# Weighted sums of a key chunk issued in two pieces of 224 queries

## The chip, the cores and the metric

The kernel runs on one core of one Trainium2 chip. The metric is device time of one whole launch in microseconds. Three runs of the kernel before gave 10486.84, 10486.08 and 10497.13 us; the median is 10486.84 us. A chip profile of one execution comes with it.

## The reference, cut to what matters

Eight images of 128 channels and 56 x 56 pixels go through three blocks, each added to its input:

- group norm, a 7 x 7 neighbourhood attention with 16 heads, and a projection;
- layer norm over channels, a full attention over all 3136 pixels with 8 heads of 16, and a projection;
- layer norm, and two small matrices (one dequantized from 4-bit codes).

The change touches only the second:

```
scores  = einsum('bhqd,bhkd->bhqk', q, k) * scale
weights = softmax(scores)
attn    = einsum('bhqk,bhkd->bhqd', weights, v)      # the "weighted sums"
```

For each image, head and query there are 3136 keys.

## The kernel before, in words

Everything is written for one core with an explicit instruction stream for each engine, ordered by semaphores. The body of the image loop is unrolled but for the strips of the neighbourhood attention.

**Units and chunks.** The full attention of an image is cut into 14 units: 2 groups of 4 heads, times 7 blocks of 448 queries. In a unit, the keys go by in 25 chunks (0 to 24) of 128 keys, the last of 64. TensorE does three kinds of work in a chunk, each with four column tiles of 32 that run side by side:

- A *score group* (`scores_turned`, L747), one for each of the 4 heads: keys on the partitions, 448 queries as columns, bf16 operands with 99 rows. It goes to one of 3 PSUM banks (6 in the last unit). Below, scores 0 to 3 are those of heads 0 to 3.
- A *maximum tile* (`max_tile`, L684), for the unit after: 448 columns, bf16, 96 rows. VectorE reduces it over the keys (`take_max`, L1112). There are 98 for a unit, so 4 in most chunks and 3 in chunks 8 and 20. Units before the last but one have them in all chunks, the last but one up to chunk 20, the last has none.
- The *weighted sum* (`weigh`, L725) of the chunk before: fp32, 128 keys as rows, 32 value columns, 448 queries as columns, one matmul for each head, each in its own column tile. A matmul in fp32 leaves two records in the trace, here called its first and its second pass. All four accumulate in PSUM bank 6 over the 25 chunks.

ScalarE takes the exponential of every score group (L937, one instruction for each head and chunk) into a buffer that the weighted sum reads. `exp_done` counts these. A score group waits until the exponential three groups earlier is done, since it takes that one's bank (L743); the first of a unit waits for every exponential of the unit before. The weighted sum waits for all four exponentials of its chunk (L721).

**Order on TensorE in a chunk of four maximum tiles** (L766 to L777): maximum 0, scores 0, maximum 1, scores 1, maximum 2, scores 2, weighted sum of the chunk before, maximum 3, scores 3. The place of the weighted sum is `weigh_at = 2` (L735), and 3 in the last unit.

**Work between chunks.** After chunk 1 TensorE spreads the sums of the unit before (`spread`, L711), after chunk 3 it projects that unit (`project`, L715), both fp32 and 448 columns; in chunk 0 ScalarE reads the finished sums (`read_sums`, L911) once `pv_done` says so, between the exponentials of heads 1 and 2. At chunk 21 VectorE finishes the maxima of the next unit (L1117) and TensorE turns them (`turn_maxima`, L705).

Of the kernel before, what the change touches and what calls it, by code (L numbers as in the profile page):

```python
# [18 lines left out]
BLK = 448  # L19
# [18 lines left out]
PRIMED = 8  # L38
# [5 lines left out]
GH = 4  # L44
GROUPS = AHEADS // GH
CHUNKS = -(-TOK // P)
# [19 lines left out]
def max_steps(c):  # L66

    at = (c - MAX_CHUNKS) % CHUNKS
    return range(-(-MAXES * at // CHUNKS), -(-MAXES * (at + 1) // CHUNKS))
# [60 lines left out]
def hybrid_block(nc, images, x, consts, qkv_wT, rpb, proj_wT, proj_b, Wq, bq, Wk, bk, Wv, bv, Wo, bo,  # L130
# [3 lines left out]
    with ExitStack() as ctx:  # L134
# [3 lines left out]
        def sem(name):  # L138
            return ctx.enter_context(nc.semaphore(name))
# [30 lines left out]
        def part(at, n, dt=F32):  # L170
            v = arena[:, at:at + n]
            return v if dt == F32 else v.bitcast(dt)
# [4 lines left out]
        VA = part(22208, 6400).rearrange("p (c h e) -> p c h e", c=CHUNKS, h=AHEADS)  # L177
# [25 lines left out]
        PS = ctx.enter_context(nc.psum_tensor("PS", [P, 8, 512], F32))  # L203
# [35 lines left out]
        st_ready, exp_done, pv_done = sem("st_ready"), sem("exp_done"), sem("pv_done")  # L239
        attn_read, sums_spread, attn_normed, attn_proj, x_updated = (  # L240
            sem("attn_read"), sem("sums_spread"), sem("attn_normed"), sem("attn_proj"),
            sem("x_updated"))
# [13 lines left out]
        def wait_parts(eng, b, g):  # L256

            eng.wait_ge(high_parts_in[g], (b + 1) * (16 * GH * len(HIGH_ROWS)))
            apart(eng)
            eng.wait_ge(parts_in[g], (b + 1) * (16 * GH * (2 * len(Q_PARTS) - len(HIGH_ROWS))))  # L260
# [9 lines left out]
        def apart(eng):  # L270


            eng.sem_inc(paced, 1)
# [5 lines left out]
        def unit_index(b, unit):  # L279
            g, i = unit  # L280
            return b * AUNITS + (g * NBLK + i)
# [4 lines left out]
        def unit_queries(unit, h, at=0, n=BLK):  # L286

            start = (unit[1] * GH + h) * BLK + at
            return slice(start, start + n)

        def attention_units(body):

            def unit_at(k):
                return (k // NBLK, k % NBLK) if 0 <= k < AUNITS else None

            for k in range(AUNITS):
                body({d: unit_at(k + d) for d in (-1, 0, 1, 2)})

        def exp_buffer(c):
            return PB[2 if c == CHUNKS - 1 else c % 2]  # L300

        LAST_UNIT = (GROUPS - 1, NBLK - 1)
# [253 lines left out]
        def _(pe):  # L556
            mm = nc.tensor.matmul
# [7 lines left out]
            with pe.Fori(0, images) as b:  # L565

                for n in range(2):
                    pe.wait_ge(gn_cols, b * 3 + (n + 1))
                    mm(PS[:, 7, n:n + 1], group_w, gn[:, 3 * n:3 * n + 1], start=True,
                       stop=True).then_inc(block_ready, 1)  # L570
# [7 lines left out]
                for j in range(NBLK):  # L578
                    wait_freed(pe, b, NK, j)
                    for c in range(4):  # L580
                        t0 = (4 * j + c) * VROW
                        m = mm(PS[0:VROW, j, c * P:(c + 1) * P], XN[:, t0:t0 + VROW], W_qkv[:, 2 * P:3 * P],
                               start=True, stop=True)
# [84 lines left out]
                for j in range(NBLK):  # L668
                    wait_freed(pe, b, AK, j)
                    for c in range(4 * j, min(4 * j + 4, CHUNKS)):  # L670
                        n = LAST if c == CHUNKS - 1 else P
                        m = mm(PS[0:n, j, (c % 4) * P:(c % 4 + 1) * P], XN[:, c * P:c * P + n], W_v[:, :],
                               start=True, stop=True)
# [15 lines left out]
                def score_for_max(unit, m):  # L689

                    u = unit_index(b, unit)
                    bank, read = max_banks()[0][m]
                    if read is not None:
                        pe.wait_ge(max_read, u * MAXES + (read + 1))
                    elif bank != 7:

                        second = unit == (0, 1)
                        last = MAXES - 1 if second else max_banks()[1][bank]
                        pe.wait_ge(max_read, u * MAXES + (last + 1 - MAXES))
                    max_tile(unit, m, bank)  # L700

                def turn_maxima(unit):
                    pe.wait_ge(row_max_in, unit_index(b, unit) + 1)
                    apart(pe)
                    nc.tensor.transpose(PS[0:QTILES, 7, 0:P], row_max[:, :], ident).then_inc(max_turned, 1)  # L705

                def spread(unit):

                    pe.wait_ge(attn_read, unit_index(b, unit) + (1 + PRIMED))
                    pe.wait_ge(x_updated, unit_index(b, unit) + PRIMED)  # L710
                    mm(PS[:, 7, 0:BLK], pick_sum, tail[:, 0, :], start=True, stop=True).then_inc(sums_spread, 1)  # L711

                def project(unit):
                    pe.wait_ge(attn_normed, unit_index(b, unit) + 1)
                    mm(PS[:, 7, 0:BLK], W_o[:, unit[0], :], normed[:, :], start=True,  # L715
                       stop=True).then_inc(attn_proj, 1)

                def weigh(unit, c):

                    e = unit_index(b, unit)  # L720
                    pe.wait_ge(exp_done, e * (GH * CHUNKS) + (GH * c + GH + PRIMED))  # L721
                    if c == 0:
                        pe.wait_ge(attn_read, e + PRIMED)
                    for h in range(GH):
                        m = mm(PS[32 * h:32 * h + 32, 6, 0:BLK], VA[:, c, unit[0] * GH + h, :],  # L725
                               exp_buffer(c)[:, h, :], start=(c == 0), stop=(c == CHUNKS - 1),
                               tile_position=(0, 32 * h))
                    m.then_inc(pv_done, 1)

                def attention_unit(units):  # L730
                    unit, after, before = units[0], units[1], units[-1]
                    e = unit_index(b, unit)
                    g = unit[0]

                    weigh_at = 2 if after is not None else GH - 1  # L735

                    def scores_turned(c, h):

                        n = LAST if c == CHUNKS - 1 else P
                        at = c * GH + h  # L740
                        banks = ST_BANKS if after is not None else ALL_ST_BANKS

                        pe.wait_ge(exp_done, e * (GH * CHUNKS) + ((at + 1 - banks if at else 0) + PRIMED))  # L743
                        if n < P:
                            apart(pe)
                        for k0 in range(0, n, 32):
                            ins = mm(PS[k0:k0 + 32, at % banks, 0:BLK], KP[0:ROWSM, g, h, c * P + k0:c * P + k0 + 32],  # L747
                                     QP[0:ROWSM, g, unit_queries(unit, h)], start=True, stop=True,
                                     tile_position=(0, k0))
                        ins.then_inc(st_ready, 1)  # L750

                    for c in range(CHUNKS):
                        later = units[1 if c < MAX_CHUNKS else 2]
                        steps = list(max_steps(c)) if later is not None else []
                        if c == MAX_CHUNKS and later is not None and later[0] != g:
                            wait_parts(pe, b, later[0])
                        if c == TAIL_DONE and before is not None and after is not None:
                            pe.wait_ge(x_updated, e + PRIMED)
                            apart(pe)

                        def maxima(n):
                            for m in steps[:n]:
                                score_for_max(later, m)
                            del steps[:n]

                        maxima(1)  # L766
                        if c == 0:

                            pe.wait_ge(shift_in, (e + 1) * (16 * 3) + 16 * PRIMED)
                        for h in range(GH):  # L770
                            scores_turned(c, h)
                            if h == weigh_at and c > 0:
                                weigh(unit, c - 1)
                            if h == weigh_at and c == 0 and before is not None:
                                weigh(before, CHUNKS - 1)
                            maxima(1)
                        maxima(len(steps))  # L777
                        if c == SPREAD_AT and before is not None:
                            spread(before)
                        if c == PROJECT_AT and before is not None:  # L780
                            project(before)
                        if c == MAX_CHUNKS and after is not None:
                            turn_maxima(after)
# [11 lines left out]
                turn_maxima((0, 0))  # L795
                pe.wait_ge(v_ones, b * 3 + 3)
                attention_units(attention_unit)
                weigh(LAST_UNIT, CHUNKS - 1)
                spread(LAST_UNIT)
                project(LAST_UNIT)  # L800

# [381 lines left out]
```

## Time and profile before

| | |
|---|---|
| median of three runs | 10486.84 us |
| profiled execution, its own time | 10482.69 us |
| its span, first to last instruction | 10480.6 us |
| TensorE matmul busy | 8999.7 us (86%) |
| VectorE busy | 8033.9 us (77%) |
| ScalarE busy | 6604.5 us (63%) |
| mean granted TensorE clock | 0.916 |

Times are microseconds from the start of the span. Busy time of TensorE counts a matmul until its modelled end, so that neighbours overlap in the records; the distance between starts tells how fast the engine goes. The queries also give "PEld", the weight loads, which overlap the matmuls. Attention units fill about 830 us of the roughly 1303 us of an image.

### The profile page before, as it was taken

Reading aid. Unit: us, or ns where it says so; the run is one execution under the profiler, and the core shown is the slowest. Engines: PE = TensorE matmul, PEld = TensorE weight load, DVE = VectorE, ACT = ScalarE, POOL = GpSimd, SP = SyncE. Lnnn points to the kernel's source line nnn. Section 1 sums busy time; section 2 is a strip of 40 time slices with the busy share of each in tenths; the row PEclk is TensorE's granted clock in tenths of the full one; section 3 lists DMA queues with packets and bytes.
Section 4 is the critical chain, followed back from the end, with each engine's and each line's share of the span. In section 5 each row is a group of like instructions: output and inputs, shape, how many; then the busy total and the mean of one; then the engine's idle time right before and its main releaser. Section 6 shows DMA issues by size and latency. Waiting matters only on the chain.

```text
span 10480.6 us, 426471 instructions
## 1 busy us (share of the span) xinstructions
PE 8999.7 (86%) x166082; PEld 4883.0 (47%) x166082; DVE 8033.9 (77%) x13861; ACT 6604.5 (63%) x13585; POOL 1650.4 (16%) x1701
## 2 busy tenths in 40 slices
PE   5699967999679996799967999679996799967999
PEld 4344453444544545444453444534445344453444
DVE  5699757997579975799757996579965799657996
ACT  3388833888338883388833888338883388734887
POOL 5200042000410004100041000410004100051000
PEclk8799987999879998799987999879998799987999
DMA  3400034000330003300033000430004300033000
GB/s 62 63 3 3 3 57 62 3 3 3 59 60 3 3 3 60 59 3 3 3 61 58 3 3 3 62 57 3 3 3 63 56 3 3 6 60 55 3 3 9
DMA packets 386155, 269.61 MB, mean 26 GB/s; under 512 B 49836, under 2 KB 377244, under 8 KB 383516
## 3 DMA queue, kind: packets, MB, share of 16 engines
q1 hardware_dynamic: 378524, 229.58, 14.0%
q0 software_dynamic: 6144, 19.28, 1.2%
q8 instruction: 1046, 17.14, 0.7%
q14 instruction: 441, 3.61, 0.1%
HBM read 144.03 MB, written 25.86 MB: 16 GB/s over the span
## 4 chain that ended last, share of the span: by engine, by line
PE 65%; issue 20%; POOL 5%; DVE 3%; SPq 3%; ACT 2%; POOLq 1%; DMA 1%; ACTq 0%; DVEq 0%
PE PS L684 21%; PE PS L747 19%; PE PS L725 19%; POOL arena L477 2%; POOL arena L467 2%; SPq L408 2%; DVE block_max L1144 2%; ACT arena L937 1%; PE PS L653 1%; PE PS L715 1%; PE PS L711 1%; PE PS L657 1%; PE PS L574 1%; PE PS L648 1%; SPq L416 0%
## 5 line engine op out<-in xcount | busy, mean ns | idle before, releaser
L1112 DVE TENSOR_REDUCE block_max<-PS 128x1 f32<-128x448 f32 x10192 | 5687.8, 617 | 494.2 <-PE PS L684 361.4
L937 ACT ACTIVATE arena<-PS 128x448 f32<-128x448 f32 (+1 forms) x11200 | 5262.6, 560 | 1161.2 <-PE PS L747 1134.2
L684 PE MATMUL PS<-KP,arena 96*32 96x448 bf16 x43904 | 4142.4, 373 | 354.5 <-DMA KP<-arena 281.0
L747 PE MATMUL PS<-arena,KP 99*32 99x448 bf16 x43904 | 4033.8, 354 | 108.3 <-ACT arena L937 73.6
L725 PE MATMUL PS<-arena 128*32 128x448 f32 x22400 | 2648.9, 540 | 19.3 <-ACT arena L937 14.8
L684 PEld LDWEIGHTS PS<-KP,arena 96*32 96x32 bf16 x43904 | 1294.7, 98 | 2024.4 <-issue 531.7
L747 PEld LDWEIGHTS PS<-arena,KP 99*32 99x32 bf16 x43904 | 1275.9, 96 | 1632.1 <-ACT arena L937 884.1
L853 ACT ACTIVATE arena<-PS 80x512 f32<-80x512 f32 (+1 forms) x896 | 442.9, 537 | 1315.1 <-PE PS L613 1312.1
L613 PE MATMUL PS<-C,arena 128*80 128x128 f32 x3136 | 582.4, 361 | 675.1 <-POOL arena L477 675.1
L526 POOL CAST shift_parts<-shift 14x128 bf16<-14x128 f32 x112 | 31.3, 279 | 5427.7 <-ACT shift L903 5427.7
L725 PEld LDWEIGHTS PS<-arena 128*32 128x32 f32 x22400 | 714.0, 110 | 360.4 <-ACT arena L937 90.6
L613 PEld LDWEIGHTS PS<-C,arena 128*80 128x80 f32 x3136 | 456.9, 155 | 751.8 <-issue 716.6
L1040 DVE TENSOR_TENSOR arena<-PS,C 128x448 f32<-128x448 f32 x224 | 139.6, 623 | 705.9 <-PE PS L623 705.8
L602 PE MATMUL PS<-arena 32*32 32x80 f32 x25088 | 528.7, 235 | 109.3 <-issue 47.9
L477 POOL TENSOR_TENSOR arena<-arena 128x1120 f32<-128x1120 f32 x224 | 461.7, 2061 | 757.3 <-DVE arena L1035 757.3
L602 PEld LDWEIGHTS PS<-arena 32*32 32x32 f32 x25088 | 484.8, 108 | 138.9 <-issue 133.2
L1144 DVE TENSOR_REDUCE block_max<-PS 128x2 f32<-128x896 f32 x336 | 388.3, 1234 | 170.4 <-PE PS L684 170.4
L472 POOL TENSOR_TENSOR arena<-arena 128x1120 f32<-128x1120 f32 x224 | 461.3, 2060 | 355.8 <-DVE arena L1029 355.8
L903 ACT ACTIVATE shift<-PS 14x128 f32<-14x128 f32 x112 | 28.0, 250 | 686.3 <-PE PS L705 686.3
L1024 DVE TENSOR_TENSOR arena<-PS,nat_bias 128x80 f32<-128x80 f32 (+3 forms) x1120 | 353.9, 382 | 119.9 <-PE PS L602 88.5
L1127 DVE TENSOR_TENSOR X<-X,PS 128x448 f32<-128x448 f32 x56 | 34.8, 621 | 481.8 <-PE PS L715 481.8
L539 POOL TENSOR_TENSOR normed<-tail 128x448 f32<-128x448 f32 x112 | 127.9, 1142 | 1623.0 <-ACT tail L919 1623.0
(98 smaller groups left out, 4893.7 us busy)
## 6 DMA issues: line engine op xcount, KB each, us to landing
arena<-vT_padded SPq DMA_DIRECT2D x1792, 70.0 KB
arena<-arena SPq DMA_DIRECT2D x384, 98.0 KB, 4.3
KP<-arena POOLq DMA_DIRECT2D x192, 98.0 KB, 8.9
KP<-arena SPq DMA_DIRECT2D x192, 98.0 KB, 4.7
arena<-in_x SPq DMA_DIRECT2D x9, 1568.0 KB, 6.7
vT_padded<-arena SPq DMA_DIRECT2D x16, 784.0 KB
out_y<-X SPq DMA_DIRECT2D x56, 224.0 KB, 2.5
arena<-shift_parts SPq DMA_DIRECT2D x336, 3.5 KB
```

The costliest lines, as they stand in the source:

```text
L472: nc.gpsimd.tensor_tensor(SC[:, k, :, :], SC[:, k, :, :], m, ALU.add).then_inc(shifted, 1)
L477: nc.gpsimd.tensor_tensor(SC[:, k, :, :], SC[:, k, :, :], r, ALU.mult).then_inc(normalised, 1)
L602: m = mm(PS[r, bk_, at * KEYS:(at + 1) * KEYS], QB[r, k, u, :], win[r, :, u * QJ:u * QJ + WJ], start=True, stop=True, tile_position=(32 * ...
L613: m = nc.tensor.transpose(PS[0:KEYS, TURN_BANKS[c], (u % 4) * P:(u % 4 + 1) * P], SC[:, k, u, :], ident)
L684: ins = mm(PS[at:at + QT, bank, 0:BLK], QP[0:ROWS, g, unit_queries(unit, h, t, QT)], KP[0:ROWS, g, h, j * BLK:(j + 1) * BLK], start=True, ...
L725: m = mm(PS[32 * h:32 * h + 32, 6, 0:BLK], VA[:, c, unit[0] * GH + h, :], exp_buffer(c)[:, h, :], start=(c == 0), stop=(c == CHUNKS - 1), ...
L747: ins = mm(PS[k0:k0 + 32, at % banks, 0:BLK], KP[0:ROWSM, g, h, c * P + k0:c * P + k0 + 32], QP[0:ROWSM, g, unit_queries(unit, h)], start= ...
L853: nc.scalar.activation(PT[0:KEYS, k, u0:u1, :].rearrange("p u e -> p (u e)"), PS[0:KEYS, TURN_BANKS[c], 0:(u1 - u0) * P], ACT.Copy).then_i ...
L937: nc.scalar.activation(exp_buffer(c)[0:n, h, :], PS[0:n, bank, 0:BLK], ACT.Exp, scale=float(ADIM) ** -0.5).then_inc(exp_done, 1)
L1024: V.tensor_tensor(SC[:, k, u0:u1, :], PS[:, bk_, at:at + m * KEYS].rearrange("p (u k) -> p u k", u=m), nat_bias[:, row_type, kind:kind + 1 ...
L1112: V.tensor_reduce(block_max[:, q, j:j + 1], PS[:, max_banks()[0][m][0], 0:BLK], AX.X, ALU.max).then_inc(max_read, 1)
L1144: V.tensor_reduce(block_max[:, m // NBLK, j0:j1], PS[:, j0:j1, 0:BLK], AX.X, ALU.max).then_inc(max_read, j1 - j0)
```

## The change

`weigh` gets a third argument, the half. Each call issues the four matmuls over 224 of the 448 columns. The waits stand ahead of the first half, the count of `pv_done` behind the second. `start` is set for the first half of chunk 0 alone, `stop` for the second half of chunk 24. The halves are issued behind scores 1 and scores 2 of the following chunk (in the last unit behind scores 2 and scores 3), each before the maximum tile that follows there. So the order in a chunk becomes: maximum 0, scores 0, maximum 1, scores 1, first half, maximum 2, scores 2, second half, maximum 3, scores 3.

```diff
-                def weigh(unit, c):
+                HALF = BLK // 2
+
+                def weigh(unit, c, half):
 
                     e = unit_index(b, unit)
-                    pe.wait_ge(exp_done, e * (GH * CHUNKS) + (GH * c + GH + PRIMED))
-                    if c == 0:
-                        pe.wait_ge(attn_read, e + PRIMED)
+                    if half == 0:
+                        pe.wait_ge(exp_done, e * (GH * CHUNKS) + (GH * c + GH + PRIMED))
+                        if c == 0:
+                            pe.wait_ge(attn_read, e + PRIMED)
+                    t = slice(half * HALF, (half + 1) * HALF)
                     for h in range(GH):
-                        m = mm(PS[32 * h:32 * h + 32, 6, 0:BLK], VA[:, c, unit[0] * GH + h, :],
-                               exp_buffer(c)[:, h, :], start=(c == 0), stop=(c == CHUNKS - 1),
+                        m = mm(PS[32 * h:32 * h + 32, 6, t], VA[:, c, unit[0] * GH + h, :],
+                               exp_buffer(c)[:, h, t], start=(c == 0 and half == 0), stop=(c == CHUNKS - 1 and half == 1),
                                tile_position=(0, 32 * h))
-                    m.then_inc(pv_done, 1)
+                    if half == 1:
+                        m.then_inc(pv_done, 1)
...
-                    weigh_at = 2 if after is not None else GH - 1
+                    weigh_at = (1, 2) if after is not None else (2, 3)
...
-                            if h == weigh_at and c > 0:
-                                weigh(unit, c - 1)
-                            if h == weigh_at and c == 0 and before is not None:
-                                weigh(before, CHUNKS - 1)
+                            if h in weigh_at and c > 0:
+                                weigh(unit, c - 1, weigh_at.index(h))
+                            if h in weigh_at and c == 0 and before is not None:
+                                weigh(before, CHUNKS - 1, weigh_at.index(h))
...
-                weigh(LAST_UNIT, CHUNKS - 1)
+                weigh(LAST_UNIT, CHUNKS - 1, 0)
+                weigh(LAST_UNIT, CHUNKS - 1, 1)
```

## Rows read from the trace of the kernel before

**Rows 1.** The page: busy time, share of the span, instructions of each engine.
```profile
PE 8999.7 (86%) x166082; PEld 4883.0 (47%) x166082; DVE 8033.9 (77%) x13861; ACT 6604.5 (63%) x13585; POOL 1650.4 (16%) x1701
```

**Rows 2.** Windows: attention of image 2 less its last unit; its last unit.
```profile
3093.00:3873.00 780.00, 770.39 (x12737) 391.89 (x12729) 708.05 (x1276) 630.02 (x1343) 31.87 (x64) 1.00 0.01 3
3876.00:3921.00 45.00, 42.88 (x564) 14.87 (x556) 4.32 (x8) 42.83 (x99) 1.14 (x1) 1.00 0.01 3
```

**Rows 3.** Timeline of an ordinary chunk: start, us, what, idle before.
```profile
3301.30 0.93 PE L725 MATMUL PS<-arena 128*32 128x448 f32 x8
3302.06 0.36 PE L684 MATMUL PS<-KP,arena 96*32 96x448 bf16 x4
3302.25 0.36 PE L747 MATMUL PS<-arena,KP 99*32 99x448 bf16 x4
3302.66 1.88 ACT L937 ACTIVATE arena<-PS 128x448 f32<-128x448 f32 x4 [0.41 <-PE PS L747]
...
3303.01 0.36 PE L747 MATMUL PS<-arena,KP 99*32 99x448 bf16 x4
3303.21 0.36 PE L684 MATMUL PS<-KP,arena 96*32 96x448 bf16 x4
3303.26 0.10 PEld L747 LDWEIGHTS PS<-arena,KP 99*32 99x32 bf16 x4
3303.40 0.36 PE L747 MATMUL PS<-arena,KP 99*32 99x448 bf16 x4
```

**Rows 4.** The same three chunks later, and the first exponential's own length (narrow window).
```profile
3309.52 1.88 ACT L937 ACTIVATE arena<-PS 128x448 f32<-128x448 f32 x4 [0.41 <-PE PS L747]
...
3302.66 0.54 ACT L937 ACTIVATE arena<-PS 128x448 f32<-128x448 f32 x1 [0.41 <-PE PS L747]
```

**Rows 5.** Timeline, chunk 1 of unit 6: TensorE and its weight loads.
```profile
3453.42 0.10 PEld L747 LDWEIGHTS PS<-arena,KP 99*32 99x32 bf16 x4 [0.24 <-ACT arena L937]
3453.42 0.37 PE L747 MATMUL PS<-arena,KP 99*32 99x448 bf16 x4
3453.62 0.93 PE L725 MATMUL PS<-arena 128*32 128x448 f32 x8
3454.57 0.36 PE L747 MATMUL PS<-arena,KP 99*32 99x448 bf16 x4
3454.86 1.02 PE L711 MATMUL PS<-tail,C 128*128 128x448 f32 x2
```

**Rows 6.** Timeline: a weighted sum on an idle TensorE (both passes), and a second pass in the stream.
```profile
1271.55 0.16 PEld L725 LDWEIGHTS PS<-arena 128*32 128x32 f32 x8 [1.38 <-ACT tail L911]
1271.55 0.58 PE L725 MATMUL PS<-arena 128*32 128x448 f32 x4 [0.94 <-ACT arena L937]
1271.95 0.56 PE L725 MATMUL PS<-arena 128*32 128x448 f32 x4
3301.68 0.55 PE L725 MATMUL PS<-arena 128*32 128x448 f32 x4
```

**Rows 7.** The page's groups: the weight loads of the weighted sums.
```profile
L725 PEld LDWEIGHTS PS<-arena 128*32 128x32 f32 x22400 | 714.0, 110 | 360.4 <-ACT arena L937 90.6
```

**Rows 8.** Timeline: end of chunk 20 and start of chunk 21.
```profile
3439.23 0.36 PE L747 MATMUL PS<-arena,KP 99*32 99x448 bf16 x4
3439.61 0.25 DVE L1117 TENSOR_REDUCE row_max<-block_max 128x14 f32<-128x98 f32 x1
3439.63 0.37 PE L684 MATMUL PS<-KP,arena 96*32 96x448 bf16 x4
```

**Rows 9.** Timeline: end of unit 5 and start of unit 6.
```profile
3449.32 0.54 ACT L937 ACTIVATE arena<-PS 64x448 f32<-64x448 f32 x1 [0.43 <-PE PS L747]
...
3449.90 0.10 PEld L747 LDWEIGHTS PS<-arena,KP 99*32 99x32 bf16 x4 [0.88 <-ACT arena L937]
3449.91 0.37 PE L747 MATMUL PS<-arena,KP 99*32 99x448 bf16 x4 [0.44 <-ACT arena L937]
```

**Rows 10.** Waits: who waited for whom, us in total, times, longest.
```profile
ACT arena L937 <- PE PS L747: 1134.2, 2620, 5.0
DVE block_max L1112 <- PE PS L684: 361.4, 1000, 4.5
```

## The prediction, made before the changed kernel was run

> **What bounds the kernel now.** The page's first part [rows 1] shows TensorE as the busiest engine. That is a mean over stages, so I went on to the windows of the attention stretch, which is all that the change touches [rows 2]. For 780 us of image 2 the matmul engine is busy 770.39 us at a granted clock of 1.00 (the 2.4 GHz level), VectorE 708 us, ScalarE 630 us. In the last unit of the image ScalarE is busy 42.83 of 45 us: there it is the bound.
>
> The timeline of an ordinary chunk shows what a full TensorE means [rows 3]. Score groups and maximum tiles start about 0.191 us apart (3302.06 to 3303.40 are seven starts, 1.34 us), close to 448 columns at 2.4 GHz, 0.187. The weighted sum takes 0.76 (3301.30 to 3302.06). From 3302.66 to 3309.52 are three chunks [rows 3, 4]: 2.287 us each, which is 8 x 0.191 + 0.756. Nothing is left between. ScalarE sits idle 0.41 in each chunk until scores 3 come; that idle time costs nothing.
>
> **The loop that lies beside the stream.** One dependence is nearly as long, and the change moves it. Scores 3 start at 3302.25, their exponential starts at 3302.66 and lasts 0.54 [rows 4], to 3303.20. Scores 2 of the next chunk need it, and their weight load starts at 3303.26, when the maximum tile ahead of it has been running for 0.05; its matmul is not late, it starts at 3303.40 on the beat. So from the start of scores 3 to the earliest weight load behind this wait: 3303.26 - 3302.25 = 1.01 us. In the old order five groups (scores 3, maximum 0, scores 0, maximum 1, scores 1) and then maximum 2, which doesn't need the exponential, lie in between: 6 x 0.191 = 1.15 us. The wait is covered with 0.14 to spare.
>
> **The change, part by part.**
>
> *The wait comes one group earlier.* The first half needs the same exponential (all four of the chunk before) and now stands ahead of maximum 2. Its slot in a full stream is 5 x 0.191 = 0.96 us behind the start of scores 3, the place where maximum 2 starts at 3303.21 [rows 3]. Its weights can't be loaded before 3303.26. Queued behind it on TensorE are its own 16 instructions, maximum 2 and scores 2; ScalarE waits for the scores, VectorE for the maximum. So TensorE runs dry for 0.05 us in each such chunk, and nothing gives it back, because TensorE has no slack.
>
> *A start on an empty engine.* With the stream broken, the load is no longer beside a matmul. Trace of before: scores 2 whose weights load at 3453.42 with nothing ahead are followed by the next group at 3453.62, 0.20 instead of 0.19 [rows 5]. For fp32 weights there is one nearer row: a weighted sum on an idle engine, passes 0.40 apart (1271.55 to 1271.95), against 0.38 in the stream (3301.30 to 3301.68) [rows 3, 6]. I take 0.023, from the 6 ns between load and matmul and 395 against 378 ns under these rounded rows. Bounds: nothing below, the whole load of 0.110 above [rows 7].
>
> *Two halves instead of one.* The columns are the same; passes go from 2 to 4 in each tile, matmuls and weight loads from 8 records to 16. In the stream a pass of 2 x 448 columns takes 0.375 to 0.378 against 0.373 by the clock, and a bf16 group 0.191 against 0.187: at most 5 ns for a change of weights. A load of 0.110 [rows 7] still fits beside a half pass of 0.19. I take 4 x 0.1905 = 0.762 for 0.756: 0.006 more. Bounds: 0 and 2 x 0.025 (below).
>
> The Trainium skill has a rule that speaks against the halves: "TensorEngine Tiling (Array Packing)", Instruction Overhead, says that each matmul has about 60 cycles of overhead. Read as something added, that is an estimate of 25 ns at 2.4 GHz for each of the two further passes, 0.05 us in a chunk, and about 140 us in all on 2800 chunks. The rows just told show 2 to 5 ns for a pass or group, so the sum doesn't use it; it is part of a rival.
>
> *Sum for an ordinary chunk.* By the loop: 1.01 + 0.023 + 0.762 + three groups (maximum 2, scores 2, maximum 3) 0.574 = 2.37 us from scores 3 to scores 3, against 2.287: **+0.084 us**. The same arithmetic on the old order gives, for a chunk whose loop does bind, 1.01 + 0.01 + 0.191 + 0.756 + 0.191 = 2.16; and its part behind the load, 3453.42 to 3454.57, is 1.15 in the rows [rows 5].
>
> **Which chunks pay.** In a unit between the first and the last two:
>
> - Chunk 3, chunks 5 to 19 and chunk 23 pay 0.084: 17 x 0.084 = 1.43. Chunk 24 pays 0.10, since its period before is 2.27.
> - Chunk 1: scores 2 wait for a late exponential in chunk 0, with maximum 2 running ahead. Now the first half takes that wait without that cover: scores 3 come 1.36 behind 3453.42, not 1.15 [rows 5]: +0.21.
> - Chunks 2, 4 and 22 have a transposition, spread or projection between scores 3 and the first half (spread starts at 3454.86 and takes about 1 us [rows 5]); the exponential is ready long before. Only the 0.006.
> - Chunk 20 would pay, but maximum 0 of chunk 21 then waits for VectorE: scores 3 of chunk 20 start at 3439.23, it would follow at 3439.42 and starts at 3439.63 [rows 8]. The 0.21 of idle time hides the 0.084. Chunk 21 then starts late enough behind the exponential.
> - Chunk 0: scores 0 wait for the last exponential of the unit before (3449.32 + 0.54, load at 3449.90 [rows 9]), so the first half finds it done.
>
> Together 1.43 + 0.10 + 0.21 + 5 x 0.006 = 1.77 us on a unit of 60.6 us, 11 such units: 19.4. Unit 0 has no spread or projection, so 19 chunks pay 0.084, with 24 and 1: 1.9. The last but one has no maximum tiles from chunk 21 on; there the wait already binds and scores 2 merely trade places with the first half, +0.02 in each of four, while chunk 20 pays: 1.7. The last unit has six banks and a full ScalarE [rows 2]; its scores lead far enough: 0.02. Per image 23.0 us, and 8 images: 184 us.
>
> Profiled execution 10482.69 (2.1 us more than its span) + 184 = 10667; the median of the runs lies 4 us above that execution: **10670 us**, 1.75% slower.
>
> **The rivals.**
>
> *The wait stays hidden (10500 us).* If the weights of the first half or of maximum 2 were fetched past the waiting instruction, or the exponential came sooner, only the 0.006 on 2800 chunks would be left: +17 us. Against it: the load of scores 2 starts 0.05 behind the exponential's end every time, not earlier [rows 3, 5]. For it: a beat of 0.05 is small, and the order before was just as tight elsewhere. The Trainium skill, "TensorE: Matmul & The Clock Gate", Part 2, says that the engine pulls weight loads ahead of matmuls in flight; if that reached past a semaphore wait, this rival would hold. The load at 3303.26, which isn't pulled past its own wait, says no [rows 3]. Chance 0.07.
>
> *The pieces cost more (about 10830 us).* The load in full on the path, 0.05 + 0.110 + 0.006 = 0.17 in each of some 1890 paying chunks, gives 321, with chunk 1 and the rest 345 us. A fixed cost of 0.025 for each further pass lands in the same region (184 + 140). Against it: the 0.40 against 0.38 on the idle engine [rows 6]. Chance 0.11.
>
> *Even feeding wins (10440 us, faster).* The gap of 0.76 in which no scores come is halved. ScalarE waits 1134 us and VectorE 361 us for TensorE [rows 10]. It would pay where TensorE itself stands idle: about 0.44 at a unit's start, 0.24 in chunk 1 and 0.21 at chunk 21 [rows 5, 8, 9], at most 0.9 in a unit, some 12 units and 8 images, 85 us; half of it gives 10440. It decides if the exponentials end more than 0.05 earlier against the stream than now. But the second half still ends ahead of scores 3 by one maximum tile as before, so their exponential comes no sooner. Chance 0.03.
>
> **How the numbers follow.** The forecast has 0.79. Its per-chunk cost lies between 0.055 (no cold start) and 0.11: 10610 to 10720 us. The range goes up into the rival with dearer pieces: 10610 to 10750; left out are the hidden wait, the faster case and most of the dearer one, under 0.2. A measurement of this kernel can't tell 0.2% (21 us) from no change. Faster 0.03, within 0.2% 0.07 (the hidden wait), slower 0.90.
>
> **What the profile of the changed kernel would show.** Starts of scores 3 (or of ScalarE's block of exponentials) 2.37 apart in ordinary chunks; the load of the first half 0.05 behind an exponential's end, with an idle time on TensorE ahead of it put down to ScalarE's L937; half passes 0.19 apart; a unit of about 62.4 us; the last unit unchanged. A chunk of 2.29 would refute the main step, one of 2.45 the price of the pieces. Chunk 21 starting its first maximum later than now would refute that VectorE's wait hides chunk 20.

## The result, and the profile after

The changed kernel takes 10674.91 us (median of four runs, 10669.02 to 10682.02); the kernel before, run beside it, 10486.46. The ratio is 1.0179, 95% interval 1.0161 to 1.0197: 188 us slower. The forecast was 10670.

The page's busy row (columns as in [rows 1]):

```profile
PE 9180.3 (86%) x188482; PEld 5359.2 (50%) x188482; DVE 8116.0 (76%) x13861; ACT 6857.5 (64%) x13585; POOL 1649.8 (15%) x1701
```

Three windows: attention of image 2 less its last unit, unit 6 alone, the last unit (columns as in [rows 2]).

```profile
3144.40:3948.00 803.60, 792.85 (x15329) 435.13 (x15325) 718.60 (x1277) 661.96 (x1345) 31.80 (x64) 1.00 0.01 3
3512.50:3574.90 62.40, 61.60 (x1197) 33.74 (x1193) 56.36 (x100) 51.26 (x104) 2.54 (x5) 1.00 0.01 3
3951.00:3995.00 44.00, 42.30 (x752) 21.06 (x748) 4.32 (x8) 42.23 (x97) 1.13 (x1) 1.00 0.01 3
```

The busy shares look as before, and busy PE even went up: here that row can't tell a good change from a bad one. The stretch of 780 us became 803.6. The clock stayed at 1.00, the 2.4 GHz level, so the small idle times cost only themselves.

The list of waits does tell. Here are the weight loads of the weighted sums (L729 in this kernel): us in total, times, longest. Before, ScalarE's exponentials ended 90.6 us of the idle time ahead of these loads [rows 7].

```profile
PEld PS L729 <- ACT arena L943: 747.8, 2272, 1.2
```

The answer to [rows 3, 4] is the timeline of an ordinary chunk, the three engines' answers one below the other. L752 are now the score groups, L729 the weighted sums, L943 the exponentials; in the experiments below the same lines shift by a few numbers. "On the beat" means: at the moment at which a full stream would have started the group.

```profile
3540.12 0.37 PE L752 MATMUL PS<-arena,KP 99*32 99x448 bf16 x4
...
3540.70 0.37 PE L684 MATMUL PS<-KP,arena 96*32 96x448 bf16 x4
3540.89 0.37 PE L752 MATMUL PS<-arena,KP 99*32 99x448 bf16 x4
3541.13 0.59 PE L729 MATMUL PS<-arena 128*32 128x224 f32 x8
3541.53 0.38 PE L684 MATMUL PS<-KP,arena 96*32 96x448 bf16 x4
3541.73 0.37 PE L752 MATMUL PS<-arena,KP 99*32 99x448 bf16 x4
3541.92 0.56 PE L729 MATMUL PS<-arena 128*32 128x224 f32 x8
3542.30 0.37 PE L684 MATMUL PS<-KP,arena 96*32 96x448 bf16 x4
3542.49 0.38 PE L752 MATMUL PS<-arena,KP 99*32 99x448 bf16 x4
...
3541.13 0.16 PEld L729 LDWEIGHTS PS<-arena 128*32 128x32 f32 x8 [0.32 <-ACT arena L943]
3541.35 0.12 PEld L684 LDWEIGHTS PS<-KP,arena 96*32 96x32 bf16 x4
...
3540.53 0.54 ACT L943 ACTIVATE arena<-PS 128x448 f32<-128x448 f32 x1 [0.22 <-PE PS L752]
```

Scores 3 start at 3540.12, their exponential runs from 3540.53 to 3541.07, the first half's weights load at 3541.13: 1.01 us behind scores 3, to the hundredth what [rows 3] gave for the old order. In a full stream its turn was at 3541.08 (3540.89 + 0.19). From its start to maximum 2 are 0.40, where the second half takes 0.38: the 0.02 of the start on an empty engine. From scores 3 to scores 3 are 2.37 (3540.12 to 3542.49).

The same over the whole trace: mean distance of the exponentials of head 3, from chunk to chunk, over units 1 to 11 of all images, worked out from the starts of the exponentials in each kernel's trace (L937 before, L943 after). The lines below the first two belong to the experiments.

```
chunk                 0      1      2      3      4     5-7    8     19     20     21     22     23     24    unit
before              3.501  2.167  3.344  2.287  3.349  2.288  2.095  2.295  2.101  2.501  2.604  2.287  2.271  60.57
after               3.508  2.454  3.364  2.371  3.363  2.372  2.181  2.371  2.180  2.444  2.613  2.370  2.355  62.40
halves, old place   3.506  2.171  3.352  2.292  3.352  2.292  2.101  2.297  2.107  2.497  2.611  2.299  2.281  60.74
maximum 2 first     3.509  2.262  3.365  2.294  3.356  2.294  2.102  2.301  2.108  2.497  2.612  2.294  2.277  60.85
short exponential   3.324  2.264  3.367  2.294  3.355  2.294  2.101  2.293  2.102  2.507  2.614  2.296  2.278  60.63
whole sum early     3.107  2.501  3.359  2.414  3.356  2.415  2.417  2.414  2.415  2.624  2.608  2.415  2.398  63.42
halves at 2 and 3   3.893  1.792  3.645  2.026  3.353  2.298  2.133  2.299  2.131  2.328  2.613  2.295  2.277  60.66
banks go on         2.890  2.167  3.346  2.288  3.349  2.288  2.096  2.290  2.100  2.501  2.605  2.287  2.275  59.95
```

### The profile page after: what moved, and what is told of

It is laid out like the page before. It is cut to its first block, busy times and chain, and to the rows that moved or that the text cites. A ratio compares the mean times of both kernels' runs of the same rounds, so it can differ in the third digit from the quotient of the medians.

```text
span 10668.8 us, 471271 instructions
## 1 busy us (share of the span) xinstructions
PE 9180.3 (86%) x188482; PEld 5359.2 (50%) x188482; DVE 8116.0 (76%) x13861; ACT 6857.5 (64%) x13585; POOL 1649.8 (15%) x1701
## 4 chain that ended last, share of the span: by engine, by line
PE 65%; issue 20%; POOL 5%; DVE 3%; SPq 3%; ACT 2%; DMA 1%; POOLq 1%; ACTq 0%; DVEq 0%
PE PS L729 20%; PE PS L684 20%; PE PS L752 18%; POOL arena L477 2%; POOL arena L467 2%; SPq L408 2%; DVE block_max L1150 2%; ACT arena L943 2%; PE PS L653 1%; PE PS L715 1%; PE PS L711 1%; PE PS L657 1%; PE PS L574 1%; PE PS L648 1%; SPq L416 0%
## 5 line engine op out<-in xcount | busy, mean ns | idle before, releaser
L1118 DVE TENSOR_REDUCE block_max<-PS 128x1 f32<-128x448 f32 x10192 | 5768.6, 620 | 599.6 <-PE PS L684 253.6
L943 ACT ACTIVATE arena<-PS 128x448 f32<-128x448 f32 (+1 forms) x11200 | 5515.4, 549 | 1097.2 <-PE PS L752 1047.0
L752 PE MATMUL PS<-arena,KP 99*32 99x448 bf16 x43904 | 4078.0, 354 | 102.5 <-ACT arena L943 68.9
L729 PE MATMUL PS<-arena 128*32 128x224 f32 x44800 | 3209.6, 357 | 39.7 <-ACT arena L943 20.3
L684 PEld LDWEIGHTS PS<-KP,arena 96*32 96x32 bf16 x43904 | 1261.4, 98 | 1485.2 <-DVE block_max L1150 283.4
L729 PEld LDWEIGHTS PS<-arena 128*32 128x32 f32 x44800 | 1217.8, 109 | 1251.3 <-ACT arena L943 747.8
L752 PEld LDWEIGHTS PS<-arena,KP 99*32 99x32 bf16 x43904 | 1281.4, 97 | 1002.3 <-ACT arena L943 173.3
```

Of the source, the lines that this page charges most:

```text
L684: ins = mm(PS[at:at + QT, bank, 0:BLK], QP[0:ROWS, g, unit_queries(unit, h, t, QT)], KP[0:ROWS, g, h, j * BLK:(j + 1) * BLK], start=True, ...
L729: m = mm(PS[32 * h:32 * h + 32, 6, t], VA[:, c, unit[0] * GH + h, :], exp_buffer(c)[:, h, t], start=(c == 0 and half == 0), stop=(c == CHU ...
L943: nc.scalar.activation(exp_buffer(c)[0:n, h, :], PS[0:n, bank, 0:BLK], ACT.Exp, scale=float(ADIM) ** -0.5).then_inc(exp_done, 1)
L1118: V.tensor_reduce(block_max[:, q, j:j + 1], PS[:, max_banks()[0][m][0], 0:BLK], AX.X, ALU.max).then_inc(max_read, 1)
```

## The experiments

My theory, from here on *the wait*: the first half's wait has lost maximum 2 as its cover; the price is the missing 0.05, the 0.02 of the start on an empty engine, and 0.006 for the pieces. The main rival, *the pieces*: more matmuls and weight loads, or their standing apart, cost the time.

**Both halves at the old place.** The changed kernel with

```diff
-                    weigh_at = (1, 2) if after is not None else (2, 3)
+                    weigh_at = 2 if after is not None else GH - 1
...
-                            if h in weigh_at and c > 0:
-                                weigh(unit, c - 1, weigh_at.index(h))
+                            if h == weigh_at and c > 0:
+                                weigh(unit, c - 1, 0)
+                                weigh(unit, c - 1, 1)
```

and the same for the call with `before`.

> Both halves are issued one behind the other where the whole weighted sum stood before (behind scores 2, in the last unit behind scores 3). The wait is where it was, covered by maximum 2. Theory of the wait: only the two further passes remain, 4 x 0.1905 for 0.756, +0.006 us a chunk, 2800 chunks: about +17 us, 10,504 us, ordinary chunks 2.293 us apart. Rival, the pieces themselves cost the time: 10,640 or more, chunks 2.35 to 2.37 apart.

Measured: ratio 1.0015 (1.0006 to 1.0024) of 10481.62, that is +16 us; the unit takes 60.74. The timeline of TensorE:

```profile
3488.33 0.38 PE L752 MATMUL PS<-arena,KP 99*32 99x448 bf16 x4
3488.52 0.95 PE L729 MATMUL PS<-arena 128*32 128x224 f32 x16
3489.28 0.39 PE L684 MATMUL PS<-KP,arena 96*32 96x448 bf16 x4
```

Sixteen records in 0.76 us, where eight took 0.76 [rows 3]. The pieces cost about the 17 us of the sum; by the interval it is between 6 and 25 us. By the rule of the Trainium skill weighed in the prediction ("TensorEngine Tiling (Array Packing)", Instruction Overhead), read as an addition, this run would have been near +140; the trace doesn't bear that reading out.

**The whole sum early.** The kernel before with

```diff
-                    weigh_at = 2 if after is not None else GH - 1
+                    weigh_at = 1 if after is not None else GH - 1
```

> The undivided weighted sum, 448 columns, is issued behind scores 1, ahead of maximum 2 (the last unit as before the change). Theory of the wait: 1.01 + 0.023 + 0.756 + 0.574 = 2.365 us a chunk, so about +170 us, 10,658 us, without any halves. Rival, the pieces cost the time: 10,487 us, chunks 2.287 apart. A rival of even spacing (the loss comes from score groups arriving late): this order has the same spread of score groups as before, so it too would say near 10,487.

Measured: 1.0292 (1.0276 to 1.0308), +306 us. Against both rivals, and far above my own 170. The timelines of ScalarE, TensorE and the weight loads tell why:

```profile
3577.58 1.85 ACT L937 ACTIVATE arena<-PS 128x448 f32<-128x448 f32 x4 [0.56 <-PE PS L747]
3580.00 1.85 ACT L937 ACTIVATE arena<-PS 128x448 f32<-128x448 f32 x4 [0.56 <-PE PS L747]
...
3579.58 0.37 PE L747 MATMUL PS<-arena,KP 99*32 99x448 bf16 x4
3579.78 0.37 PE L684 MATMUL PS<-KP,arena 96*32 96x448 bf16 x4
3579.97 0.37 PE L747 MATMUL PS<-arena,KP 99*32 99x448 bf16 x4
...
3578.61 0.16 PEld L725 LDWEIGHTS PS<-arena 128*32 128x32 f32 x8 [0.33 <-ACT arena L937]
```

ScalarE's idle time of 0.56 now stands ahead of head 2, not of head 3 (0.41 in [rows 3]). Scores 2 and 3 are 0.39 apart (3579.58, 3579.97), but ScalarE starts an exponential only about 0.44 behind the one before it (four in 1.85, of which the last takes its full 0.54). So the exponential of head 3, which everything waits for, queues behind that of head 2 and starts 0.47 behind its scores instead of 0.41. The chunk becomes 2.414 instead of 2.365. Where a chunk has three maximum tiles, nothing stands between scores 2 and 3 and the loop through ScalarE stays 2.417 long: the 0.19 that such a chunk was shorter before is lost too. I had left ScalarE's queue out of the loop since it is busy only 81% there. No run changes that queue alone; this account is read from the timelines. In the changed kernel the second half stands between scores 2 and 3 and keeps them 0.76 apart: the split costs less than moving the undivided sum would.

**Halves behind scores 2 and scores 3**, the changed kernel with `weigh_at = (2, 3)` in every unit.

> Halves behind scores 2 and scores 3 in every unit. The first half waits in the place where the whole sum did. Theory of the wait: ordinary chunks 2.293 apart as in the run with both halves at the old place; but in chunk 0 the end of the unit before comes one maximum tile and one score group later (0.38), ScalarE's reading of the sums waits for it and scores 1 and 2 of chunk 1 wait for ScalarE: +0.38 x 12 units x 8 images = +37 us; with +17 for the passes and about 5 in the last unit 10,545 us. Rival, the pieces or the parting of them cost the time: 10,640 or more.

Measured: 1.0016 (1.0006 to 1.0025), +17 us: no rival's 10,640, but not my 10,545 either. The start of a unit behaves as I had said and then gives nearly all of it back: chunk 0 takes 0.39 more, chunk 1 0.37 less, chunk 2 0.30 more, chunk 3 0.26 less (table). Chunk 21 takes another 0.17 less. In chunk 1 only half of the sum is left between the wait and scores 3:

```profile
3458.16 0.37 PE L752 MATMUL PS<-arena,KP 99*32 99x448 bf16 x4
3458.36 0.55 PE L729 MATMUL PS<-arena 128*32 128x224 f32 x8
3458.74 0.36 PE L684 MATMUL PS<-KP,arena 96*32 96x448 bf16 x4
3458.93 0.36 PE L752 MATMUL PS<-arena,KP 99*32 99x448 bf16 x4
```

From scores 2, which waited, to scores 3 are 0.77; in [rows 5] they are 1.15. The loop is 1.01 + 0.77 = 1.78 long, and 1.79 is measured. I had counted a delay once and not asked what the shorter loop gives back.

**Maximum 2 ahead of the first half.** One instruction group swaps places with another; everything else of the change stays:

```diff
                             scores_turned(c, h)
+                            if h == weigh_at[0]:
+                                maxima(1)
...
-                            maxima(1)
+                            if h != weigh_at[0]:
+                                maxima(1)
```

> As the changed kernel, but maximum 2 is issued ahead of the first half instead of behind it: maximum 1, scores 1, maximum 2, first half, scores 2, second half, maximum 3, scores 3. Halves, their parting and the place ahead of scores 2 stay; only the cover of the wait comes back (its slot is 6 x 0.191 = 1.15 us behind scores 3, the exponential allows 1.01). Theory of the wait: ordinary chunks 2.293 apart; +17 for the passes, +0.10 in chunk 1 of 96 units (+9), +5 in the last units: 10,517 us. Rival, pieces or their parting: 10,650 or more, chunks 2.35 to 2.37 apart.

Measured: 1.0035 (1.0022 to 1.0047), +37 us, where 31 were expected. Ordinary chunks are back at 2.29 to 2.31. TensorE and its weight loads:

```profile
3506.07 0.36 PE L684 MATMUL PS<-KP,arena 96*32 96x448 bf16 x4
3506.26 0.55 PE L729 MATMUL PS<-arena 128*32 128x224 f32 x8
3506.65 0.36 PE L752 MATMUL PS<-arena,KP 99*32 99x448 bf16 x4
...
3506.11 0.26 PEld L729 LDWEIGHTS PS<-arena 128*32 128x32 f32 x8
```

The load of the first half still comes late (3506.11, with maximum 2 running since 3506.07), but beside a matmul: the half starts on the beat. This swap alone takes away 151 of the 188 us.

**A shorter exponential.** The changed kernel with

```diff
-                               exp_buffer(c)[:, h, t], start=...
+                               exp_buffer(c)[:, h, slice(0, HALF) if h == GH - 1 else t], start=...
...
-                            nc.scalar.activation(exp_buffer(c)[0:n, h, :], PS[0:n, bank, 0:BLK],
+                            w = BLK // 2 if h == GH - 1 else BLK
+                            nc.scalar.activation(exp_buffer(c)[0:n, h, 0:w], PS[0:n, bank, 0:w],
```

> The changed kernel, but the exponential of head 3 covers only 224 of 448 queries, and head 3's second half of the weighted sum reads the first half's values: half of that head's exponentials are left out. TensorE's instructions, order and waits are the same. That exponential ends about 0.19 us sooner, more than the 0.08 that the first half comes late. Theory of the wait: TensorE's stream closes, ordinary chunks 2.293 us apart, the time falls to about 30 us above the kernel before, 10,513. Rival (the pieces, their loads, or where they stand cost the time): chunks stay at 2.37, time stays near 10,670.

Measured: 0.9981 (0.9972 to 0.9991), 20 us faster than the kernel before. TensorE's program is that of the changed kernel, and its chunks are 2.293 to 2.297 long. ScalarE with head 3's exponential, the weight load of the first half, and TensorE:

```profile
3472.34 0.36 ACT L944 ACTIVATE arena<-PS 128x224 f32<-128x224 f32 x1 [0.22 <-PE PS L752]
...
3472.75 0.27 PEld L729 LDWEIGHTS PS<-arena 128*32 128x32 f32 x8
...
3472.69 0.38 PE L752 MATMUL PS<-arena,KP 99*32 99x448 bf16 x4
3472.88 0.57 PE L729 MATMUL PS<-arena 128*32 128x224 f32 x8
```

The exponential ends at 3472.70, the load follows 0.05 later, and scores 1, started at 3472.69, cover it: the half starts on the beat. The time went below my 10,513 because less exponential also shortens what ScalarE bounds: the last unit, 44.2 us for 47.7 (28 us in all), and chunk 0, 3.32 for 3.51 (18 us). Together 46 us, and 10,513 less 46 is 10,467; the median is 10,465.5.

**One wait in chunk 1.** The changed kernel without

```diff
-                        if c == 0:
-                            pe.wait_ge(attn_read, e + PRIMED)
```

> The changed kernel without the second wait (attn_read) ahead of the weighted sum of chunk 0; the first wait already implies it, since ScalarE reads the old sums before the exponentials of heads 2 and 3. In the changed kernel the weights of that first half load 0.12 after the exponential's end, in other chunks 0.05. If the second wait instruction, which can't be passed until the first is satisfied, makes the 0.07, chunk 1 goes from 2.454 to 2.385 us and the whole by 96 x 0.07 = 7 us. If the late load has another cause (ScalarE's reading itself, the bank), chunk 1 stays at 2.454.

Chunk 1 took 2.380 us. The exponential of head 3 in chunk 0 and the half's load, in the changed kernel and then in this one:

```profile
3514.52 0.97 ACT L943 ACTIVATE arena<-PS 128x448 f32<-128x448 f32 x2
...
3515.61 0.16 PEld L729 LDWEIGHTS PS<-arena 128*32 128x32 f32 x8 [0.40 <-issue]
```

```profile
3519.74 0.97 ACT L941 ACTIVATE arena<-PS 128x448 f32<-128x448 f32 x2
...
3520.76 0.16 PEld L727 LDWEIGHTS PS<-arena 128*32 128x32 f32 x8 [0.33 <-ACT arena L941]
```

0.12 behind the exponential's end (3515.49) with two waits, 0.05 (3520.71) with one. A satisfied wait isn't free where the one ahead of it has just been met: about 0.07 us. The 0.07 is the mean over 88 units as well (2.454 to 2.380). Only one run gave a time, 10668.31, too few to see 7 us in.

**The last unit as before the change**, halves together behind scores 3 there.

> The changed kernel, but in the last unit both halves stand together behind scores 3. The last unit takes 47.7 us in the changed kernel and 47.1 before. If scores 3 standing behind the wait of the first half delays spread and project by one group, chunks 2 and 4 go back from 3.46 and 2.74 to 3.26 and 2.54 us, and the unit to 47.1: 5 us of the whole. If the halves themselves do it, they stay. All other units as in the changed kernel.

Chunks 2 and 4 took 3.268 and 2.544, the unit 47.11 us (mean of eight): as expected. Its one time, 10663.19, can't show the 5 us. TensorE around the spread after chunk 1, changed kernel first:

```profile
3951.18 0.38 PE L729 MATMUL PS<-arena 128*32 128x224 f32 x4
3951.49 1.02 PE L711 MATMUL PS<-tail,C 128*128 128x448 f32 x2
```

```profile
3952.36 1.02 PE L711 MATMUL PS<-tail,C 128*128 128x448 f32 x2
```

The exponential of head 3 in chunk 1 starts at 3951.41 and 3952.48: spread comes 0.08 behind it there, 0.12 ahead of it here. Scores 3 had moved behind a wait that they don't need, and spread, on which ScalarE waits, stood behind them.

**A version that beats both.** The idle times that I had listed as the most that any order could win have one large member, the 0.44 ahead of scores 0 of a unit [rows 9]. It comes from starting each unit at bank 0, the bank of the last exponential of the unit before. The kernel before, with

```diff
+        def bank_turn(units):
+            if units[1] is None or units[-1] is None:
+                return None
+            return (units[0][0] * NBLK + units[0][1]) * GH * CHUNKS % ST_BANKS
...
-                        pe.wait_ge(exp_done, e * (GH * CHUNKS) + ((at + 1 - banks if at else 0) + PRIMED))
+                        turn = bank_turn(units)
+                        free = at + 1 - banks if at or turn is not None else 0
+                        pe.wait_ge(exp_done, e * (GH * CHUNKS) + (free + PRIMED))
```

and `(turn or 0) + at` for `at` in the bank of the matmul and of the exponential.

> The kernel before (undivided sums at the old place), with the three banks of the score groups continuing their turn from unit to unit instead of starting again at bank 0; so scores 0 of a unit wait for the exponential three groups earlier and not for the last of the unit before. Units 1 to 12 of an image; first and last as before. The theory that TensorE is the bound and only its own idle time counts: the idle 0.44 us ahead of scores 0 (up to 0.6 counted from the beat) go, in 96 units: 42 to 58 us less, about 10,435 us. Rival: the wait for the shift's DMA or ScalarE's reading of the sums takes the place of the one removed, and the time stays at 10,482.

Measured: 0.9940 (0.9927 to 0.9954) of 10487.54, 10426.75 us. Scores 3 of chunk 24 and scores 0 of the next unit:

```profile
3434.53 0.36 PE L755 MATMUL PS<-arena,KP 99*32 99x448 bf16 x4
...
3434.91 0.39 PE L755 MATMUL PS<-arena,KP 99*32 99x448 bf16 x4
```

They are 0.38 apart, with one maximum tile between. (A score group of chunk 24 has only two matmuls, so these rows of four also hold two of a neighbouring group.) Chunk 0 takes 2.89 for 3.50, 0.61 x 96 units = 59 us, and the rest of the unit is as before.

## Why the prediction was right

- *Full TensorE, covered wait.* Right. The wait's length of 1.01 us read off the old order held to the hundredth in the new one; the swap of maximum 2 and the short exponential each closed the stream again by one end of the same wait.
- *Rival "the wait stays hidden".* Fell. No load passes a waiting one in these rows: the weights of maximum 2, which depend on no exponential, load at 3541.35, behind the half's at 3541.13. What the Trainium skill says in "TensorE: Matmul & The Clock Gate", Part 2, of weight loads pulled ahead of matmuls fits the second of them, which stands 0.18 ahead of its own matmul (3541.53); no load in these rows gets past a semaphore wait, its own or that of a load before it.
- *Rival "the pieces cost more".* Fell by the halves at the old place, +16 us.
- *Rival "even feeding wins".* Fell: with the wait covered again and the spacing kept, the time is still 37 us above before. The gain was never in the spacing of scores; that idle time of TensorE can be won is shown by the last run, by taking it directly.
- *Which chunks pay.* 0.084 forecast, 0.082 to 0.085 measured in chunks 3, 5 to 7 and 23; chunk 24 0.084 for 0.10. Chunk 20 paid 0.079 and chunk 21 gave 0.057 back through VectorE's wait: 0.022 for the 0.006 of the sum. Counted from the exponential of head 3 in chunk 19, the first maximum tile of chunk 21 starts 0.02 later than before: by the sign that the prediction named, VectorE's wait hid most of what chunk 20 pays, not all. Late in the unit the kernel before took up to 2.295, so the difference is 0.076 there.
- *Two terms were too small.* Chunk 1: +0.29, not +0.21, by the second wait instruction (shown), 7 us. The last unit: +0.6 us, not 0.02 (shown), 5 us. Against them stands that late chunks of the kernel before were slightly longer than 2.287.
- *Unit 0 was too large.* It paid 1.50 (chunks 1 to 24), not 1.9. The sum gave its chunk 1 the +0.21 of the late exponential, but in unit 0 ScalarE has no sums of a unit before to read in chunk 0, and that chunk became 0.07 shorter (3.254 for 3.325). That is about 3 us the other way.
- *A rounding.* The terms of the ordinary chunk add up to 2.369, which is 0.082 above 2.287; the 0.084 comes from the missing 0.055, the 0.023 and the 0.006. Over the paying chunks the two differ by 4 us.

From the first to the last exponential of an image are 854.6 us (mean of eight), 830.5 before: 24.1, where the sum had 23.0. The spans differ by 188.2 us; 193 of it is attention, and the 5 that the other stages lack can't be told from noise. So it is in part luck that the sum's 184 lies within 4 us of the 188 measured, and the forecast within 5 us of the median; the mechanism is not luck.

## What to carry to other kernels

Where an engine is full, look for the second loop beside its stream, through another engine and back, and write down what covers its wait; moving a consumer one slot earlier can cost what is missing of the cover in every iteration, though no work is added. Add each engine on that loop with its queue, not its busy share: at 81% busy ScalarE still lengthened the loop of the undivided early sum. And a full engine gains only from its own idle times: list them with their count before choosing an order.

## What the runs showed of the hardware

- Halving fp32 matmuls of 448 columns (32 weight columns, four tiles) costs next to nothing: 16 records in 0.76 us, as 8 before, and 6 to 25 us on 5600 further passes.
- A weighted sum whose weights load on an idle engine costs 0.02 us more than one in the stream, though its load's record is 0.11 long.
- A second semaphore wait that is already satisfied delays the weight load by about 0.07 us, where the first wait has only just ended (0.12 against 0.05).
- In the last unit ScalarE's chunk is 1.69 to 1.70 us at first and 1.747 later, in every kernel here with full exponentials: from chunk 11 or 12 on, or from chunk 8 on in the kernels with parted halves there. I have not found the cause.
